# Denominators of three sixteen-head attention stages from products with ones, and one of two copies moved to ScalarE

## What is computed

```python
qkv = x @ w_qkv + b_qkv
q, k, v = jnp.split(qkv, 3, axis=-1)
q = q.reshape(B, T, N_HEADS, dh)
k = k.reshape(B, T, N_HEADS, dh)
v = v.reshape(B, T, N_HEADS, dh)
scores = jnp.einsum('bqhd,bkhd->bhqk', q, k) / jnp.sqrt(jnp.float32(dh)).astype(x.dtype)
probs = jax.nn.softmax(scores, axis=-1)
ctx = jnp.einsum('bhqk,bkhd->bqhd', probs, v).reshape(B, T, D)
return ctx @ w_o + b_o
```

## Time and profile before

| | before |
|---|---|
| time, median of 3 runs | 5619.62 us (5614.51 to 5624.86) |
| the profiled execution's own time | 5612.67 us |
| its span in the profile | 5610.9 us |
| TensorE busy | 4515.5 us (80%) |
| VectorE busy | 3488.2 us (62%) |
| ScalarE busy | 2539.5 us (45%) |
| GpSimd busy | 1838.9 us (33%) |
| mean granted TensorE clock | 0.91 |
| l0a, first to last turn of the scales | 60.7 to 262.9 us |
| l2x, the same | 2818.6 to 3021.7 us |
| l3f, the same | 4864.0 to 5071.2 us |

### The profile page before, as it was taken

The page is one execution under the profiler, slowest core; times in us unless marked ns, Lnnn a source line. Parts: engine busy times, 40 slices in busy tenths (PEclk is TensorE's granted clock), DMA queues, the critical chain, the costliest instruction groups (busy, mean ns, idle before and its releaser), DMA issues. The chain is left out here.

```text
span 5610.9 us, 100171 instructions
## 1 busy us (share of the span) xinstructions
PE 4515.5 (80%) x31417; PEld 3055.8 (54%) x31417; DVE 3488.2 (62%) x7389; ACT 2539.5 (45%) x9241; POOL 1838.9 (33%) x2278
## 2 busy tenths in 40 slices
PE   7848847767769799973896899998999755496999
PEld 5524424444448677752564455555777623265776
DVE  6836539878866556557786666665566568784111
ACT  6826612223324377751395222222677522493443
POOL 4314338856654322232652000000333235450000
PEclk8969979978879899986997999999999988697999
DMA  5040150010000000000001000000000022000000
GB/s 72 4 40 28 25 43 0 0 38 0 0 9 2 18 4 4 4 3 3 7 12 54 1 0 0 1 0 15 1 0 0 0 91 80 33 2 1 0 0 15
DMA packets 261025, 85.83 MB, mean 15 GB/s; under 512 B 204106, under 2 KB 253523, under 8 KB 258932
## 3 DMA queue, kind: packets, MB, share of 16 engines
q1 hardware_dynamic: 260740, 82.43, 7.2%
HBM read 73.63 MB, written 15.07 MB: 16 GB/s over the span
## 5 line engine op out<-in xcount | busy, mean ns | idle before, releaser
L2698 ACT ACTIVATE l2f_e_sg<-l2f_e_G 128x512 f32<-128x512 f32 x288 | 172.1, 597 | 629.0 <-PE l2f_e_U L2664 629.0
L2674 PEld LDWEIGHTS l2f_e_Y<-l2f_wd,l2f_e_h 128*128 128x128 f32 x2304 | 280.2, 191 | 214.7 <-issue 199.2
L2716 DVE TENSOR_TENSOR l2f_e_h<-l2f_e_sg,l2f_e_U 128x512 f32<-128x512 f32 x288 | 198.3, 688 | 315.4 <-ACT l2f_e_sg L2698 275.9
L2674 PE MATMUL l2f_e_Y<-l2f_wd,l2f_e_h 128*128 128x128 f32 x2304 | 318.9, 281 | 22.3 <-DVE x_sbuf L2724 14.4
L2674 PEld LDWEIGHTS l3f_e_Y<-l3f_w,l3f_e_h 128*128 128x128 f32 x2048 | 267.7, 192 | 121.6 <-issue 115.1
L2724 DVE SCALAR_TENSOR_TENSOR x_sbuf<-l2f_e_Y,l2f_share,x_sbuf 128x128 f32 x1152 | 322.8, 343 | 3.7 <-DVE x_sbuf L2724 3.7
L2662 PE MATMUL l2f_e_G<-l2f_XT,l2f_wg 128*128 x576 | 296.8, 597 | 30.9 <-DVEq L2711 30.9
L2724 DVE SCALAR_TENSOR_TENSOR x_sbuf<-l3f_e_Y,l3f_share,x_sbuf 128x128 f32 x256 | 72.1, 345 | 383.3 <-PE l3f_e_Y L2674 383.3
L2694 ACT ACTIVATE l3f_e_h<-l3f_e_G,l3f_b 128x512 f32<-128x512 f32 x256 | 175.9, 687 | 263.9 <-PE l3f_e_G L2662 263.9
L2664 PE MATMUL l2f_e_U<-l2f_XT,l2f_wu 128*128 x576 | 295.1, 594 | 0.0
L2039 POOL MEMSET l3a_Kexp<- 128x4096 f32 x1 | 3.5, 3511 | 878.1 <-POOLq L107 878.1
(11 more groups left out here) (613 smaller groups left out, 12858.4 us busy)
## 6 DMA issues: line engine op xcount, KB each, us to landing
l3x_Mb<-l3x_dram_max SPq DMA_DIRECT2D x32, 512.0 KB, 3.3
l0f_ew<-in_l0f_ew SPq DMA_DIRECT2D x1, 4096.0 KB
l3f_w<-in_l3f_w SPq DMA_DIRECT2D x2, 2048.0 KB
l2f_wg<-in_l2f_wg SPq DMA_DIRECT2D x1, 2304.0 KB
l2f_wu<-in_l2f_wu SPq DMA_DIRECT2D x1, 2304.0 KB
l2f_wd<-in_l2f_wd SPq DMA_DIRECT2D x1, 2304.0 KB
l0v_CT<-in_ctxT_rows SPq DMA_DIRECT2D x1, 2048.0 KB
x_sbuf<-in_x_tokens SPq DMA_DIRECT2D x1, 2048.0 KB, 15.5
```

The costliest lines, as they stand in the source:

```text
L2674: mm = nc.tensor.matmul(Y[e % 2][:, k * P:(k + 1) * P], h[:, n % 2, k * P:(k + 1) * P], w2[:, n, :], start=(c == 0 and k == 0), stop=(c == ...
L2698: nc.scalar.activation(sg[:, n % 2, :], G[n % 2][:, :], ACT.Silu).then_inc(silu_done, 1)
L2716: nc.vector.tensor_tensor(h[:, n % 2, :], sg[:, n % 2, :], U[n % 2][:, :], ALU.mult).then_inc(h_done, 1)
```

## The change

In `head_attention` the sums of the probabilities are no longer taken by ScalarE beside the exponentials. `sum_keys` issues sixteen more products, the same turned probabilities against a constant of ones and zeros (`C.one4`, which `phi_attention` already uses), into the columns of `N` where the turned scale stood. `den`, `wide_r`, `invert`, `widen`, `turn_scale` and `copy_scale` go. `divide` takes the reciprocal of 128x128 sums from PSUM into `rT`, waits for it, and multiplies. Of the two copies of turned probabilities VectorE keeps half 0; half 1 is copied by ScalarE, between `copy_qk(b+2)` and the exponentials of (b, 1). Both count on the same semaphore `pt_done`, for which `turn` and `sum_keys` wait.

```diff
-                def turn_scale(b):
-                    wait(pe, wide_done, b + 1)
+                def sum_keys(b):
                     wait(pe, x_done, b)
-                    nc.tensor.transpose(N[:, P:2 * P], wide_r[:, :], C.ident).then_inc(rt_mm, 1)
-
-                def sum_keys(b):
-                    wait(pe, rt_done, b + 1)
                     wait(pe, pt_done, 2 * b + 2)
                     for j in range(4):
                         for q in range(4):
                             rows = slice(32 * q, 32 * q + 32)
-                            mm = nc.tensor.matmul(N[rows, 0:P], Vx[:, b % 4, j * P + 32 * q:j * P + 32 * q + 32],
+                            nc.tensor.matmul(N[rows, 0:P], Vx[:, b % 4, j * P + 32 * q:j * P + 32 * q + 32],
+                                             PT[:, b % 2, 4 * q + j, :], start=(j == 0), stop=(j == 3))
+                    for j in range(4):
+                        for q in range(4):
+                            rows = slice(32 * q, 32 * q + 32)
+                            mm = nc.tensor.matmul(N[rows, P:2 * P], C.one4[:, j * P + 32 * q:j * P + 32 * q + 32],
                                                   PT[:, b % 2, 4 * q + j, :], start=(j == 0), stop=(j == 3))
                     mm.then_inc(pv_mm, 1)
...
-                def copy_turned(b, n):
+                def copy_turned(b):
                     wait(dve, pv_mm, b - 1)
-                    wait(dve, tp_mm, 2 * b + n + 1)
-                    nc.vector.tensor_copy(PT[:, b % 2, 8 * n:8 * n + 8, :].rearrange("p h k -> p (h k)"),
-                                          TP[:, :]).then_inc(pt_done, 1)
-
-                def invert(b):
-                    wait(dve, exp_done, 2 * b + 2)
-                    nc.vector.reciprocal(den[:, b % 2, :], den[:, b % 2, :]).then_inc(r_done, 1)
+                    wait(dve, tp_mm, 2 * b + 1)
+                    nc.vector.tensor_copy(PT[:, b % 2, 0:8, :].rearrange("p h k -> p (h k)"), TP[:, :]).then_inc(pt_done, 1)
...
                     wait(dve, y_mm, b)
+                    nc.vector.reciprocal(rT[:, :], N[:, P:2 * P]).then_inc(r_done, 1)
+                    wait(dve, r_done, b + 1)
                     nc.vector.tensor_tensor(oT[:, :], N[:, 0:P], rT[:, :], ALU.mult).then_inc(ot_done, 1)
...
-                def exps(b, n, first=0, last=8):
+                def exps(b, n):
                     wait(act, max_done, 2 * b + n + 1)
                     wait(act, tp_mm, 2 * b + n - 1)
-                    wait(act, wide_done, b - 1)
-                    for h in range(8 * n + first, 8 * n + last):
+                    for h in range(8 * n, 8 * n + 8):
                         ins = nc.scalar.activation(Pr[:, h, :], S[:, h * P:(h + 1) * P], ACT.Exp,
-                                                   bias=nmx[:, b % 2, h:h + 1], accum_out=den[:, b % 2, h:h + 1])
-                    if last == 8:
-                        ins.then_inc(exp_done, 1)
+                                                   bias=nmx[:, b % 2, h:h + 1])
+                    ins.then_inc(exp_done, 1)
+
+                def copy_turned(b):
+                    wait(act, pv_mm, b - 1)
+                    wait(act, tp_mm, 2 * b + 2)
+                    nc.scalar.copy(PT[:, b % 2, 8:16, :].rearrange("p h k -> p (h k)"), TP[:, :]).then_inc(pt_done, 1)
...
                     if span(b + 2):
                         copy_qk(b + 2)
+                    if span(b - 1):
+                        copy_turned(b - 1)
                     if span(b):
-                        exps(b, 1, 0, 3)
-                    if span(b - 1):
-                        copy_scale(b - 1)
-                    if span(b):
-                        exps(b, 1, 3, 8)
+                        exps(b, 1)
```

More of the change, by code:

```diff
@@ L634, in head_attention @@
         nmx = sb("nmx", [P, 2, 16])
-        den = sb("den", [P, 2, 16])
         Pr = sb("Pr", [P, 16, P])
         PT = sb("PT", [P, 2, 16, P])
-        wide_r = sb("wide_r", [P, P])
         rT = sb("rT", [P, P])
@@ L642, in head_attention @@
         (zeros_done, xnt_mm, xnt_done, qkv_mm, qk_done, v_done, kexp_done, s_mm, max_done, exp_done, tp_mm, pt_done,
-         pv_mm, r_done, wide_done, rt_mm, rt_done, ot_done, y_mm, x_done, biased, ctx0, ctx1, ctx2, ctx3) = sems(25)
+         pv_mm, r_done, ot_done, y_mm, x_done, biased, ctx0, ctx1, ctx2, ctx3) = sems(22)
         ctx_in = [ctx0, ctx1, ctx2, ctx3]
@@ L674, in spread @@
                     pool.tensor_tensor(Kexp[:, b % 2, :, :], keys, bcast_in(C.km4, P), ALU.mult).then_inc(kexp_done, 1)
[L676 to L680, removed]
                 def drain(b):
@@ L686, in step @@
                 def step(b):
-                    if span(b - 1):
-                        widen(b - 1)
                     if span(b + 2):
@@ L765, in step @@
                         scores(b + 1, 0)
-                    if span(b - 1):
-                        turn_scale(b - 1)
                     if span(b):
@@ L817, in step @@
                         less_max(b, 1)
-                    if span(b - 1):
-                        invert(b - 1)
-                        copy_turned(b - 1, 1)
                     if span(b - 2):
@@ L827, in step @@
                     if span(b):
-                        copy_turned(b, 0)
+                        copy_turned(b)
                     if span(b + 5):
@@ L868, in copy_normed @@
                                              scale=affine[0]).then_inc(xnt_done, 1)
[L870 to L873, removed]
                 def step(b):
```

## The result

The changed kernel takes 5692.82 us (median, 5690.89 to 5699.59, 4 runs) against 5621.58 us before (5614.51 to 5624.86, 4 runs). The ratio is 1.0131, 95% interval 1.0113 to 1.0148: 71 us slower. The forecast was 5695 us.

The account below looks back on a forecast made before the run. ScalarE was taken to set the pace, TensorE close behind. Steps of 7.21 us in l0a and 7.46 in l2x and l3f add 74 us, stage ends 1.5: +75 us, forecast 5695 us, range 5655 to 5720.

Parts of the forecast that it names:

- ScalarE leads before, TensorE close behind: In l0a before the change, ScalarE sets the pace and TensorE has only about 0.3 us of room in 6.56.
- TensorE's floor of 7.05 us: TensorE's step after the change: 6.56 - 0.16 + 0.04 + 0.62 = 7.06 us, taken as 7.05, within 6.95 to 7.1.
- The stall: TensorE idles before the second turn, waiting for ScalarE's turned copy: 0.20 us in l0a, 0.45 us in l2x and l3f.
- the upper of my two bounds: Wait from ScalarE's copy to TensorE's second turn: 0.15 us by the trace before, possibly less; 0.10 was taken.
- VectorE and the reciprocal: VectorE loses a 1.195 us copy, gains a 0.953 us reciprocal; load at most 5.6 us a block, its extra wait delaying no one.
- The rival that emptying PSUM is the bound: Sharing PSUM copies pays: ScalarE's 5.65 us sets the period in the three stages, about 5536 us in total; chance 0.04.
- The sum: Averages of 7.21 us in l0a, 7.46 in l2x and l3f: 74 us over 31 periods, +75 us with stage ends.
- the correction from the steady step to the average over a stage: Averages over a stage's start and end lie 0.04 us below the steady step, as in the kernel before.
- The ends of the stages: At each stage's end ones and reciprocal add, the old scale chain goes: +0.5 us a stage, estimated, 1.5 in all.

## Why the prediction was right

- *ScalarE leads before, TensorE close behind.* Shown from both sides: a little room on ScalarE brought 15 us and made TensorE the bound in l0a; more work on ScalarE, without the other edits, cost 70 us.
- *TensorE's floor of 7.05 us.* In the middle of l0a the changed kernel's step is 7.27 us with a second turn at 1.32 us behind the scores. With the copy moved ahead it is 1.06, and the turn costs 0.93 instead of 0.90 to the next start: 7.27 - 0.26 + 0.03 = 7.04 us; the step measured in that run is 7.05. The 0.89 us of the ones came back as 0.86 when they were taken away.
- *The stall.* Forecast 0.20 us in l0a and 0.45 in the others, measured 0.19 and 0.43 as idle entries; by starts the second turn is 0.26 us late in l0a and 0.49 in l2x. The wait from ScalarE to TensorE is 0.15 us, the upper of my two bounds, and not the 0.10 I took. The copy lasts 1.01 us, as the two smaller sizes gave it. The Trainium skill's figure (ScalarE: Activation LUTs, What ACT_TABLE_LOAD costs), 1.04 us, is 0.03 us too long here; the measured time decides.
- *VectorE and the reciprocal.* 0.957 us each, and no effect on the time when it goes. Two readings of the prediction were too favourable here, without consequence: VectorE carries 125.2/160 x 7.27 = 5.7 us a block and not "at most 5.6", and the output projection needs the quotient 1.2 us after it is made (in l0a the multiply ends at 167.70, the projection starts at 168.93), not almost 4 us later.
- *The rival that emptying PSUM is the bound.* It falls. Giving half of the turned copies to ScalarE cost 70 us by itself, where ScalarE was full, and 33 us on top of the denominators, 30 of which were its place in the queue. VectorE, from which the copy was taken, was not the bound in any of these runs. The Trainium skill (TensorEngine Tiling (Array Packing), PSUM Bottleneck) advises using both ScalarE and VectorE for it; no run here was faster for doing so.
- *The sum.* The steady steps came out 0.02 us above the forecast (7.27 and 7.52 against 7.25 and 7.50). The term that was off is the correction from the steady step to the average over a stage: I took the 0.04 us of the kernel before, and it is 0.12 and 0.16. The last steps of a stage have no projections and no scores left, which shortens a step that TensorE sets and hardly shortens one that ScalarE sets: in l0a the last three are 6.28, 6.28 and 5.22 us instead of 7.27 after the change, and 6.50, 6.47 and 5.40 instead of 6.57 before. That makes 66 us instead of 74 for the steps. The ends of the stages cost 3 us instead of 1.5, and the medians differ by 71 instead of 75. That the total came within 3 us of 5695 is in part luck: the median of before rose by 2 us with a fourth run (5621.58 against 5619.62), and the rest of the program varies by more than that.

What stays open: why the work outside the three stages took between 4940 and 4958 us in these executions. Sharing the denominators between accumulators and ones, so that neither engine is full, wasn't tried.

## What to carry to other kernels

Before moving work from the leading engine to another, read how full that other engine is from the distances between its starts, not from busy shares: here the second engine had 0.3 us of room in 6.56, got 0.8 net of what was taken from it, and the leader's 1 us of relief was lost. A copy moved into another engine's queue must be placed by what the instruction ahead of it waits for; the same 1.01 us instruction cost 30 us more behind a waiting copy than ahead of it. And a dearer way to make one quantity can pay when it frees the layout: the ones lost 39 us as a replacement for the accumulators, and the kernel won 117 us when they allowed a layout without turns and their copies, at the price of leaving out the maxima.

## What was not expected

Moving only the copy, and making the whole change, cost the same within the intervals (1.0125 and 1.0131), with ScalarE full in the one and TensorE, but for the stall, full in the other. A time alone would not tell them apart; one row of busy time does.
